# Head logits from stacked operands: full-array matmuls, one PSUM bank at a time

## What is computed

```python
x = x + tanh(g_xattn[0]) * L0_xattn(layernorm(x), ctx)   # relu attention
x = x + tanh(g_ffn[0])   * L0_ffn(layernorm(x))          # 512 -> 1024 -> 1024 -> 256, weights +-1
x = x + tanh(g_xattn[1]) * L1_xattn(layernorm(x), ctx)   # the part around the change
x = x + tanh(g_ffn[1])   * L1_ffn(layernorm(x))          # shared expert + 64 routed experts, top 8
...
# L1_xattn: the memory is the context row with the highest score of each token
qp = q @ Wq.T; idx = argmax(qp @ kv.T); mem = kv[idx]; mk, mv = split(mem @ Wkv.T)
logits = einsum('bhld,bmd->bhlm', heads(qp, 16), mk) / 4  # 16 heads of 16, one key head
out = softmax(logits) @ mv; return merge(out) @ Wc.T
```

## Time and profile before

| | |
|---|---|
| median of three runs | 1842.63 us (1838.82 to 1842.83) |
| the profiled execution: its time, its span | 1847.19 us, 1845.2 us |
| busy share of the span: PE, PE weight load, DVE | 91%, 77%, 72% |
| ACT, POOL | 52%, 55% |
| granted TensorE clock, mean over the span | 0.969 |
| chain that ended last: PE, DMA, DVE, ACT | 69%, 8%, 7%, 4% |
| its share in the line of `c_lg`, L1193 | 4% |

### The profile page before, as it was taken

The page is one execution under the profiler, slowest core; times in us unless marked ns, Lnnn a source line. Parts: engine busy times, 40 slices in busy tenths (PEclk is TensorE's granted clock), DMA queues, the critical chain, the costliest instruction groups (busy, mean ns, idle before and its releaser), DMA issues.

```text
span 1845.2 us, 51326 instructions
## 1 busy us (share of the span) xinstructions
PE 1681.7 (91%) x17188; PEld 1418.1 (77%) x17188; DVE 1330.1 (72%) x4610; ACT 964.5 (52%) x2789; POOL 1023.1 (55%) x1627
## 2 busy tenths in 40 slices
PE   5799999999999999999999999999999998458785
PEld 4588888888788888878888888888888876347775
DVE  5477777777677777777777787777777865436554
ACT  3455555555555555555555555555555544214443
POOL 4125666666566666655666666666666653345555
PEclk9899999999999999999999999999999998579999
DMA  7411111111111111101111111111010012138886
GB/s 235 141 17 48 50 46 44 47 51 39 30 30 28 37 26 43 29 21 30 33 30 26 33 26 26 26 27 26 25 30 21 21 57 74 48 96 215 197 198 136
DMA packets 134336, 108.98 MB, mean 59 GB/s; under 512 B 70559, under 2 KB 123753, under 8 KB 134296
## 3 DMA queue, kind: packets, MB, share of 16 engines
q1 hardware_dynamic: 100504, 89.30, 16.7%
q0 software_dynamic: 33792, 19.17, 5.9%
HBM read 51.63 MB, written 111.84 MB: 89 GB/s over the span
## 4 chain that ended last, share of the span: by engine, by line
PE 69%; DMA 8%; DVE 7%; issue 6%; ACT 4%; another core or an unknown queue 4%; POOL 2%; SPq 0%; POOLq 0%; DVEq 0%; ACTq 0%
PE bank L1133 22%; PE bank L1031 8%; DMA out<-ey,aid 6%; PE bank L1117 6%; PE ps_yo L1031 4%; PE ps_m L1031 4%; PE ps_lg L1193 4%; PE ps_lg L1031 3%; PE ps_yo L1149 3%; PE ps_tr L1057 3%; PE ps_m L1231 2%; PE ps_pt L1031 2%; PE ps_pt L1208 2%; ACT xr L774 2%
## 5 line engine op out<-in xcount | busy, mean ns | idle before, releaser
L637 POOL DMA_INDIRECT table<-xs,slot x496 | 505.4, 1019 | 199.3 <-issue 171.8
L1133 PE MATMUL bank<-h_h,held 128*128 128x256 f16 x2048 | 267.6, 274 | 2.8 <-DVE h_l L1616 1.7
L1133 PE MATMUL bank<-h_l,held 128*128 128x256 f16 x2048 | 266.9, 273 | 0.7 <-issue 0.7
L579 POOL TENSOR_TENSOR pool_pad<-pad_in 128x1 f32<-128x1 f32 x382 | 75.0, 196 | 325.4 <-PE ps_tr L1240 163.8
L838 ACT ACTIVATE p<-ps_lg,rmax 128x77 f32<-128x77 f32 x1024 | 235.5, 351 | 7.3 <-DVE rmax L1681 7.0
L1133 PEld LDWEIGHTS bank<-h_l,held 128*128 128x128 f16 x2048 | 201.2, 98 | 25.0 <-issue 1.1
L1133 PEld LDWEIGHTS bank<-h_h,held 128*128 128x128 f16 x2048 | 193.7, 98 | 25.4 <-issue 3.3
L1616 DVE SCALAR_TENSOR_TENSOR h_l<-bank,h_h 128x512 f16<-128x512 f32 x256 | 175.0, 684 | 27.8 <-ACT h_h L824 22.4
L653 POOL TENSOR_TENSOR rs<-nt,minushalf 128x2 f32<-128x2 f32 x128 | 92.5, 722 | 163.5 <-DVE nt L1578 152.4
L844 ACT ACTIVATE pt_h<-ps_pt 128x384 f16<-128x384 f32 x128 | 62.8, 491 | 189.0 <-PE ps_pt L1208 189.0
L741 POOL DMA_INDIRECT out<-ey,aid x64 | 98.7, 1542 | 97.1 <-DVE aid L1963 57.4
(11 more groups left out here) (279 smaller groups left out, 4574.9 us busy)
## 6 DMA issues: line engine op xcount, KB each, us to landing
ew<-in_e_wts SPq DMA_DIRECT2D x48, 384.0 KB
table<-xg SPq DMA_DIRECT2D x8, 1284.0 KB, 15.9
xg<-table SPq DMA_DIRECT2D x64, 160.5 KB
xs<-xr SPq DMA_DIRECT2D x31, 320.0 KB, 2.7
x<-in_x SPq DMA_DIRECT2D x32, 256.0 KB
...
```

The costliest lines, as they stand in the source:

```text
L637: g.indirect_dma_start(out=table, out_offset=bass.IndirectOffsetOnAxis(ap=slots[:, t, k:k + 1], axis=0), in_=rows[:, t, :], in_offset=None ...
L1133: ins = mm(two(bank[j % 2])[:, m % 2, :], wb1[:, k, m * P:(m + 1) * P], hp[:, k, :], start=(i == 0 and k == 0), stop=(i == 1 and k == FK - 1))
```

## The change

The four products of a bank become one contraction over 128 partitions. A stack `qst` [128, 4 pairs, 2, 256] holds, for each pair of heads (32 feature rows), the high queries, the low queries, the high queries again and a constant 61440; `kst` [128, 2, 77] holds the high keys, the high keys, the low keys and the mask (0 or -61440). Per batch, the first quarter of the stack is filled by four transfers on SyncE's queue (`stack`), the second by four VectorE copies, the third by four ScalarE copies (both `c_stack`); the last is set once. `c_lg(i)` for i = 0 to 7 fills one bank, with two matmuls of 154 columns, and `c_max(i)`, `c_exp(i)` work by bank. `p32` has two buffers, r runs over (head half, token half), and the transposes are 2 and 3 blocks instead of 3 and 2. The orders of steps on TensorE, ScalarE and VectorE are rewritten. `eth` and `ega` of the expert loop move into `q32` to make room, GpSimd builds other constants, and `a_q`, the scatter pacing and `take_keys` wait on the same points under new counts. On ScalarE the new order of `first` is `d_gu(3)`, `b_l0(0)`, `d_ac(2)`, `d_ac(3)`, `c_qp`, `b_l0(1..3)`, `c_stack`, `d_route`, `c_exp(0)`, `c_exp(1)`, `b_l1(0)`, `c_exp(2)`, `c_pt(0)`, `c_vb`, `c_pt(1)`, `c_exp(3)`, `c_exp(4)`, `c_pt(2)`, `c_pt(3)`, `c_exp(5)`, `c_pt(4)`, `c_pt(5)`, `c_exp(6)`, `c_exp(7)`, `c_pt(6)`, `c_pt(7)`, `b_l1(1)`.

```diff
 
 
 PC = -(-HC * S2 // P)
-TURNED = [range(0, 3), range(3, PC)]
+TURNED = [range(0, 2), range(2, PC)]
...
+            def stack(b):
+                sp.wait_ge(qp_hi, b + 1)
+                w(sp, lg_rdy.sem, lg_rdy.nth(7, b - 1))
+                for p in range(HP):
+                    sp.dma_start(qst[0:Q4, p, :, :], qp_h[p * Q4:(p + 1) * Q4, :, :]).then_inc(qst_in, 16)
 
...
-                hm = halfmask[:, :].unsqueeze(2).to_broadcast([P, HB, S2])
+                g.tensor_tensor(kr_m[:, :], kr_h[:, :], lowpart[:, 0:1].to_broadcast([P, S2]), ALU.mult).then_inc(kb_ok, 1)
+                pool.wait_ge(kb_ok, 3 * b + 1)
+                g.tensor_tensor(kr_x[:, :], kr32[:, :], kr_m[:, :], ALU.subtract).then_inc(handoff, 1)
                 pool.wait_ge(handoff, b + 1)
-                g.tensor_tensor(kb_h[:, :, :], kr_h[:, :].unsqueeze(1).to_broadcast([P, HB, S2]), hm, ALU.mult).then_inc(kb_ok, 1)
-                g.tensor_tensor(kb_l[:, :, :], kr_l[:, :].unsqueeze(1).to_broadcast([P, HB, S2]), hm, ALU.mult).then_inc(kb_ok, 1)
+                n = 3 * Q4
+                g.tensor_tensor(kst[0:n, :, :], kr_x[0:n, :].unsqueeze(1).to_broadcast([n, PH, S2]),
+                                pairmask[0:n, :].unsqueeze(2).to_broadcast([n, PH, S2]), ALU.mult).then_inc(kb_ok, 2)
 
 
...
+            def c_stack(b):
+
+                act.wait_ge(qp_hi, b + 1)
+                w(act, lg_rdy.sem, lg_rdy.nth(7, b - 1))
+                for p in range(HP):
+                    last = a.activation(qst[2 * Q4:3 * Q4, p, :, :], qp_h[p * Q4:(p + 1) * Q4, :, :], ACT.Copy)
+                last.then_inc(qst_a, 1)
+
...
+            def c_lg(i, b):
+
+                r, g_ = divmod(i, 2)
+                c, t = divmod(r, T2)
+                if i == 0:
                     pe.wait_ge(sv_ev, b + 2 if not isinstance(b, int) else min(b + 2, NB))
-                    pe.wait_ge(kb_ok, 2 * b + 2)
+                    pe.wait_ge(kb_ok, 3 * b + 3)
                     pe.wait_ge(mrow_ok, b + 1)
-                else:
-                    pe.wait_ge(p_ok.sem, p_ok.nth(r - 1, b))
+                    pe.wait_ge(qst_a, b + 1)
+                    pe.wait_ge(qst_ok, b + 1)
+                    pe.wait_ge(qst_in, 64 * b + 64)
+                elif r:
+                    pe.wait_ge(p_ok.sem, p_ok.nth(i - 2, b))
                 tt = slice(t * P, (t + 1) * P)
-
-                for i, (keys, queries) in enumerate([(mrow, None), (kb_h, qp_h), (kb_l, qp_h), (kb_h, qp_l)]):
-                    for g_ in range(2):
-                        rows = slice(g_ * 64, (g_ + 1) * 64)
-                        ins = mm(ps_lg[:, g_, 0:HB * S2], row0[rows, :] if queries is None else queries[rows, c, tt], keys[rows, :, :],
-                                 start=(i == 0), stop=(i == 3))
+                for at in range(HP // 2):
+                    ins = mm(ps_lg[:, g_, at * PH * S2:(at + 1) * PH * S2], qst[:, g_ * (HP // 2) + at, c, tt], kst[:, :, :], start=True, stop=True)
                 ins.then_inc(lg_rdy.sem, 1)
 
             def c_pt(k, b):
 
-                if k % 2 == 0:
-                    pe.wait_ge(p_ok.sem, p_ok.nth(k // 2, b))
+                pe.wait_ge(p_ok.sem, p_ok.nth(k, b))
                 if k >= 2:
                     pe.wait_ge(pt_lo_ok.sem, pt_lo_ok.nth(k - 2, b))
...
                     b_l0(3, n)
-                if on(c):
-                    c_cnt(c)
                 if on(d):
                     d_dn(1, d)
                 if on(c):
+                    c_cnt(c)
+                if on(n):
+                    b_l1(0, n)
+                if on(c):
                     c_lg(0, c)
+                    c_lg(1, c)
+                if on(n):
+                    b_l1(1, n)
+                if on(c):
                     c_vb(c)
-                if on(n):
-                    b_l1(0, n)
-                    b_l1(1, n)
-                if on(c):
-                    c_lg(1, c)
+                    c_lg(2, c)
                     c_pt(0, c)
-                    c_pt(1, c)
                 if on(m) and early(m):
                     transposes(0, m, xn[0])
                 if on(n):
                     b_l1(2, n)
+                if on(c):
+                    c_pt(1, c)
+                    c_lg(3, c)
+                    c_lg(4, c)
+                if on(n):
                     b_l1(3, n)
                 if on(c):
-                    c_lg(2, c)
+                    c_lg(5, c)
                     c_pt(2, c)
+                    c_av(0, c)
+                    c_lg(6, c)
+                    c_pt(3, c)
+                if on(n):
+                    b_l1(4, n)
                 if on(d):
                     d_cp(d)
                 if on(c):
-                    c_pt(3, c)
-                    c_av(0, c)
-                if on(n):
-                    b_l1(4, n)
-                if on(c):
-                    c_lg(3, c)
+                    c_lg(7, c)
                     c_pt(4, c)
                     c_pt(5, c)
                     c_av(1, c)
                 if on(n):
                     b_l1(5, n)
                 if on(c):
+                    c_pt(6, c)
                     c_av(2, c)
-                    c_pt(6, c)
                     c_pt(7, c)
 
             def second(n):
@@ -1361,17 +1396,18 @@
                 if on(m):
                     a_q(m)
                     a_kv(m)
-                    a_vals(m)
                 if on(c):
                     c_av(3, c)
                 if on(m):
+                    a_vals(m)
+                if on(c):
+                    c_att(c)
+                if on(n):
+                    b_l1(6, n)
+                if on(c):
+                    c_wc(c)
+                if on(m):
                     a_s(m)
-                if on(c):
-                    c_att(c)
-                if on(n):
-                    b_l1(6, n)
-                if on(c):
-                    c_wc(c)
                 if on(n):
                     b_l1(7, n)
...
+            def c_stack(b):
+
+                dve.wait_ge(qp_lo, b + 1)
+                w(dve, lg_rdy.sem, lg_rdy.nth(7, b - 1))
+                for p in range(HP):
+                    last = v.tensor_copy(qst[Q4:2 * Q4, p, :, :], qp_l[p * Q4:(p + 1) * Q4, :, :])
+                last.then_inc(qst_ok, 1)
...
             def c_counts(b):
                 dve.wait_ge(cnt_rdy, b + 1)
-                v.tensor_scalar(mrow[:, :, :], ps_tr[:, 2 * P:2 * P + S2].unsqueeze(1).to_broadcast([P, HB, S2]),
-                                0.0, NEG, ALU.is_equal, ALU.mult).then_inc(mrow_ok, 1)
+                far = slice(3 * Q4, P)
+                v.tensor_scalar(kst[far, :, :], ps_tr[far, 2 * P:2 * P + S2].unsqueeze(1).to_broadcast([Q4, PH, S2]),
+                                0.0, -FAR, ALU.is_equal, ALU.mult).then_inc(mrow_ok, 1)
+
+            def c_values(b):
                 cch.did(v.tensor_copy(cnt[:, :], ps_tr[0:S2, 3 * P:3 * P + 1]))
                 cch.wait()
                 w(dve, vb_rdy, b)
...
-            def c_max(r, b):
-
-                dve.wait_ge(lg_rdy.sem, lg_rdy.nth(r, b))
-                lg = ps_lg[:, :, 0:HB * S2].rearrange("p g (h k) -> p g h k", k=S2)
+            def c_max(i, b):
+
+                r, g_ = divmod(i, 2)
+                dve.wait_ge(lg_rdy.sem, lg_rdy.nth(i, b))
                 if r > 1:
-                    dve.wait_ge(p_ok.sem, p_ok.nth(r - 2, b))
+                    dve.wait_ge(p_ok.sem, p_ok.nth(i - 4, b))
                 else:
-                    w(dve, p_ok.sem, p_ok.nth(r + 2, b - 1))
-                v.tensor_reduce(rmax[r % 2][:, :].rearrange("p (g h) -> p g h", g=2), lg, AX, ALU.max, negate=True).then_inc(z_ok.sem, 1)
+                    w(dve, p_ok.sem, p_ok.nth(i + 4, b - 1))
+                v.tensor_reduce(rmax[r % 2][:, g_ * HB:(g_ + 1) * HB], ps_lg[:, g_, 0:HB * S2].rearrange("p (h k) -> p h k", k=S2),
+                                AX, ALU.max, negate=True).then_inc(z_ok.sem, 1)
 
...
                 if on(d):
+                    d_max(d)
                     d_gu(3, d)
                     d_ac(1, d)
-                    d_ac(2, d)
                 if on(n):
                     b_l0(0, n)
                 if on(c):
                     c_qp(c)
                 if on(d):
+                    d_ac(2, d)
+                if on(n):
+                    b_l0(1, n)
+                if on(d):
                     d_ac(3, d)
-                if on(n):
-                    b_l0(1, n)
                 if on(c):
                     c_argmax(c)
                 if on(n):
                     b_l0(2, n)
-                if on(c):
+                    b_l0(3, n)
+                if on(c):
+                    c_stack(c)
                     c_counts(c)
-                if on(n):
-                    b_l0(3, n)
-                if on(d):
-                    d_max(d)
-                if on(c):
+                    c_values(c)
                     c_max(0, c)
+                    c_max(1, c)
```

(67 more changed lines are left out.)

121 lines of the change are left out of this document (63 added, 58 removed).

## The result

The changed kernel takes 1849.78 us (median of 13 runs, 1848.13 to 1852.35), the kernel before beside it 1841.92: a ratio of 1.0038, 95% interval [1.0027, 1.0048]. It is 0.4% slower, where 1782 us was forecast. The profiled execution has a span of 1849.9 us at a granted clock of 0.972.

What follows compares the result with a forecast made beforehand. PE, busy 98% of the loop, was taken as the bound. Terms summed to -1.77 us a batch, -53 over 30 batches; late norms -2 and tail -5 made -60: 1787 from the profiled 1847.2, 1782 off the median, range 1760 to 1814.

Steps and rivals of the forecast that it cites:

- The matmul term, -1.77: PE's `c_lg` steps: 2.92 us a batch removed, 1.05 of new matmuls and 0.10 for a gap added, net -1.77.
- The removed stalls, -0.70: PE's stalls of 0.46 and 0.24 us before `c_pt(4)` and `c_pt(5)` go, -0.70 us a batch.
- Filling the stack, 0: Transfers, ACT copies and DVE copies that fill the stack before `c_lg(0)` are all hidden, costing 0.
- Rivals A and D: A: stack late on DVE, +1.2 us a batch, 1818 us, 13%. D: transfers land late, about 1905 us, 6%.
- I walk the new orders with 0.05 to 0.2 us for each handover: Softmax chain by bank: start and end times of PE, DVE and ACT steps, allowing 0.05 to 0.2 us per handover.
- `c_pt(1)` needs `ps_yo` free: At `c_pt(1)`: `d_x4` ends at 755.65 and PE arrives at 755.8, so no stall was added.
- `c_lg(7)` was to cost 0.20: PE's wait at `c_lg(7)`: due at 761.43 while `c_exp(5)` ends at 761.65, +0.20 us a batch.
- `a_sv`, +0.30: Second half of the batch: `a_sv` waits for DVE's `a_l`, now behind `c_x3` and layer norm sums, +0.30 us.
- `b_l1(0)`, +0.15: Ahead of `c_lg(0)`: PE waits at `b_l1(0)` for the low half of `b_l0(3)`, a new stall of +0.15 us.
- Rival B: Chain by bank tighter than walked: PE stops 1.0 us more a batch at `c_lg(5)` to `c_lg(7)`, 1812 us, 12%.
- The tail, -5: In `first(32)`, where nothing covers the softmax, two banks in turn shorten the steps: -5 us, bounds 0 and -8.
- Late norms, -2: Two late layer norms in the loop hurt less, as `transposes(3)` comes 0.9 us of PE work later: about -1 each.

Runs made afterwards that it cites:

- e17: Kernel before with DVE's `c_norm(0)` moved behind low halves 2 and 3, the edit of e8 again, where signals are not held: 1792.43 us, ratio 1.0005.
- e14: The changed kernel, unaltered, run again where signals are not held: 1773.38 us against 1792.23 for the kernel before, ratio 0.9905.
- e8: Kernel before with DVE's `c_norm(0)` moved behind low halves 2 and 3, where signals are held: 1811.24 us against 1838.98 unedited.
- e5: Changed kernel with `c_vb` moved behind `c_lg(2)` and `c_pt(0)` on PE: 1796.03 us against 1838.98 for the kernel before.
- e7: Changed kernel with the move of e5 and `c_pt(3)` ahead of `c_av(0)` on PE: 1793.28 us against 1838.98 for the kernel before.
- e12: e7 with `c_max(5)` ahead of `d_choose` on DVE, where signals are not held: 1764.84 us against 1789.83 for the kernel before.

## Why the prediction was wrong

- **The matmul term, -1.77.** The mechanism and the size of the step were right: `c_lg` costs 1.08 us a batch by start to start, against 1.05 forecast, with no gaps. PE's period outside stalls over 0.15 us fell from 46.22 us (e17, which has none) to 45.87 - 0.24 - 0.69 - 0.17 = 44.77 us (e14): -1.45. The other 0.3 us are small gaps, each under 0.15, that the sum had at nothing.
- **The removed stalls, -0.70.** Right where signals are held (e8: 28 us), nothing where they are not (e17).
- **Filling the stack, 0.** Rivals A and D did not happen. The DVE copies took 0.28 us each for 0.25 said (one of the four 0.51 in 15 of 25 batches of the first trace). The transfers took 2.46 us to issue for 1.6 said, and the last landed 3.4 to 3.9 us before `c_lg(0)`. ScalarE's copies, 0.63 us each for 0.5, are what comes last: in e14 they end at 725.14, PE's wait for them ends at 725.18, and `c_lg(0)` starts at 725.51 after 0.24 us idle. In the first trace the late `b_l1(0)` hides this.
- **The failed step: "I walk the new orders with 0.05 to 0.2 us for each handover."** Two handovers of PE took 1.37 and 2.02 us. "`c_pt(1)` needs `ps_yo` free" was to cost nothing and costs 1.18; `c_lg(7)` was to cost 0.20 and costs 1.56. Together +2.54 us a batch. The period was to be 45.69 us and is 48.10, 2.41 us more, which over 30 batches is 72 us of a miss of 68. e5 and e7 took the held part of both away without touching the stack (0.41 to 0.74 us stay at `c_lg(7)`), and e7 came to 1793 us, where its kernel before took 1839.
- **The other new stalls.** `a_sv`, +0.30, was 0.17; `b_l1(0)`, +0.15, was 0.23. `c_lg(7)` without the hold is 0.69, not 0.20; `chosen`, which stands ahead of it on DVE, takes 0.8 us longer behind GpSimd than alone, enough for the difference, and in e12, where `chosen` is prompt and `c_max(5)` no longer stands behind it, the stall is gone.
- **Where no signal is held.** The sum without the 0.70 of old stalls is -1.07 us a batch, and 46.22 to 45.87 is -0.35. Of the 0.72 us between, 0.32 are the small gaps and 0.40 are stalls of 1.10 us (0.24, 0.69, 0.17) in place of 0.70. So without held signals the gain is 19 us, where the sum without the old stalls has 39.
- **Rival B** had one of the two places (`c_lg(5)` to `c_lg(7)`) and the effect, PE stopped by the chain by bank, and its sign, PE idle on Exp by over 0.5 us a batch, stood in the trace; it was priced at 1.0 us from slow handovers all round, where two handovers were very slow.
- **The tail, -5.** From one `c_vb` to the next, the last interval is 39.54 us in e14 and 46.37 in e17, the one before it 49.67 and 48.22: -5.4.
- **Late norms, -2.** Right. The two of the kernel before stopped PE 3.21 and 2.15 us; at the same places the changed kernel loses 2.06 and 1.37 us (ahead of `b_l2(0)`), 1.9 us less, and the clock, 0.50 in the earlier trace rows, stays at 1.00.

What stays open: why a signal is held beside some indirect transfers and not others, and why two chips hold none. No run here tells. That it belongs to the chip and not to the time of the run is argued, not shown, from two things: one of the chips was met in two groups of runs and took 1789.8 and 1792.5 us for the kernel before, and within a group all executions of it lie within 0.7%.
